# Values held stationary and turned weights streamed, with the weights normalised before their turn, in a six-layer windowed-attention kernel

## The reference, cut to what matters

```
q, k, v = split(shift_tokens(x) @ Wqkv)          # 16 heads of 64
q, k = l2norm(q) * qs, l2norm(k) * ks ; rotary with scale
sim  = einsum('bhwie,bhwje->bhwij', q, k2) * 8   # 8 windows of 32 queries, 64 keys: own window and the one before
attn = softmax(where(mask, -max, sim))
out  = einsum('bhwij,bhwje->bhwie', attn, v2)
x    = out @ Wo + x
x    = (a * gelu(gate)) @ W2 + b2 + x            # of a layer norm of shift_tokens(x), hidden 341
```

## Time and profile before

| quantity | value |
|---|---|
| time, median of 3 runs | 1986.11 us (1985.73 to 1987.9) |
| profiled execution, its own time | 1993.02 us |
| its span | 1991.2 us |
| one full body (start of S0 to the next) | 34.06 us |
| TensorE's granted clock, mean | 0.97 of 2.4 GHz |

### The profile page before, as it was taken

One profiled execution on the slowest core, in us unless ns is written; L12 is line 12 of the kernel. 1 busy time (PEld: TensorE's weight loads), 2 busy tenths in 40 slices (PEclk: granted clock), 3 DMA queues, 4 the chain that ended last, 5 costly groups with the idle time before them and its releaser, 6 DMA issues.

```text
span 1991.2 us, 84866 instructions
## 1 busy us (share of the span) xinstructions
PE 1858.3 (93%) x35408; PEld 1303.1 (65%) x35408; DVE 1589.7 (80%) x3092; ACT 1045.7 (53%) x1879; POOL 903.9 (45%) x1231
## 2 busy tenths in 40 slices
PE   6888858899999999999999999999999999999996
PEld 3444424676767777777767677776767676777674
DVE  5565557788988888888888888888889888888883
ACT  2444423455555656555555556565556555465553
POOL 1000015364554646464555546464645555464640
PEclk7898888999999999999999999999999999999997
DMA  2001006556566656566565666565665646564650
GB/s 69 10 7 64 0 3 100 83 80 102 74 122 109 94 82 94 117 95 108 78 104 72 122 109 94 82 93 117 93 110 76 106 71 124 104 95 83 91 91 22
DMA packets 73332, 166.87 MB, mean 84 GB/s; under 512 B 16592, under 2 KB 23504, under 8 KB 72400
## 3 DMA queue, kind: packets, MB, share of 16 engines
q0 software_dynamic: 36864, 100.71, 37.9%
q1 hardware_dynamic: 36432, 65.68, 12.7%
HBM read 20.57 MB, written 1.05 MB: 11 GB/s over the span
## 4 chain that ended last, share of the span: by engine, by line
PE 69%; DVE 9%; issue 7%; DMA 2%; ACT 0%; DVEq 0%; POOL 0%; POOLq 0%; ACTq 0%
PE ps L997 14%; PE ps L1033 8%; PE ps L1087 7%; PE ps L1107 6%; PE ps L1057 6%; PE ps L1141 5%; PE ps L1009 5%; PE ps L1070 4%; PE ps L1100 3%; DVE big L815 3%; PE ps L1131 3%; PE ps L1021 3%; DVE big L825 2%; DMA big<-big 2%; PE ps L1048 2%
## 5 line engine op out<-in xcount | busy, mean ns | idle before, releaser
L477 POOL DMA_DIRECT2D big<-big x768 | 607.0, 1497 | 62.4 <-DVE big L807 43.9
L564 ACT ACTIVATE big<-ps 128x512 f32<-128x512 f32 x384 | 228.4, 595 | 587.6 <-PE ps L997 540.0
L997 PE MATMUL ps<-big,wn_sb 128*128 128x256 f32 x1536 | 411.2, 396 | 17.5 <-issue 14.9
L815 DVE TENSOR_TENSOR big<-big,ps 128x512 f32<-128x512 f32 x384 | 249.6, 680 | 93.2 <-PE ps L1021 82.8
L997 PEld LDWEIGHTS ps<-big,wn_sb 128*128 128x128 f32 x1536 | 275.4, 192 | 69.6 <-issue 16.5
L468 POOL TENSOR_TENSOR big<-big 128x512 f32<-128x512 f32 x96 | 123.4, 1285 | 360.8 <-ACT big L581 360.8
L804 DVE TENSOR_TENSOR big<-ps,tab 128x512 f32<-128x512 f32 x384 | 262.0, 682 | 11.0 <-ACT big L564 10.9
L807 DVE TENSOR_TENSOR big<-ps,tab 128x512 f32<-128x512 f32 x384 | 259.0, 674 | 0.0
L1141 PE MATMUL ps<-big,wo_sb 128*128 128x256 f32 x768 | 214.5, 382 | 0.0
L443 POOL COPY big<-xs 64x256 f32 x144 | 79.2, 550 | 263.5 <-DVE xs L843 257.6
L1033 PE MATMUL ps<-wn_sb,big 128*64 128x512 f32 x768 | 182.0, 611 | 0.7 <-DVE big L807 0.7
(11 more groups left out here) (146 smaller groups left out, 2917.1 us busy)
## 6 DMA issues: line engine op xcount, KB each, us to landing
big<-big POOLq DMA_DIRECT2D x768, 128.0 KB, 5.0
big<-big SPq DMA_DIRECT2D x96, 256.0 KB
big<-big SPq DMA_DIRECT2D x96, 192.0 KB
wn_sb<-in_wn SPq DMA_DIRECT2D x6, 1024.0 KB, 10.0
wn_sb<-in_wn SPq DMA_DIRECT2D x6, 512.0 KB, 6.1
wo_sb<-in_wo SPq DMA_DIRECT2D x6, 512.0 KB, 4.0
w_sb<-in_w SPq DMA_DIRECT2D x6, 341.0 KB, 3.0
w_sb<-in_w SPq DMA_DIRECT2D x6, 192.0 KB, 3.3
```

Of the source, the lines that this page charges most:

```text
L477: eng.dma_start(rot[to:to + 32, at:at + 4, :], src[32 * r:32 * r + 32], accum_op=ALU.add).then_inc(added[i], 16)
L564: eng.activation(sq[:, two, :], ps[:, i % 2, :].rearrange("p (a t) -> p a t", a=2), ACT.Square).then_inc(sq_d, 1)
L815: eng.tensor_tensor(hat[:, two, :], rot[:, two, :], ps[:, i % 2, :].rearrange("p (a t) -> p a t", a=2), ALU.mult).then_inc(hat_d, 1)
L997: mm = eng.matmul(ps[:, k % 2, a * T:a * T + T], wn_sb[:, u * P:u * P + P], sT, start=True, stop=True)
```

## The change

`W` swaps its operands. A value tile of 64 keys by 64 columns is now stationary, and 32 queries of the turned weights are moving; there are still 32 matmuls a step, now of the shape 64 rows by 64 columns with 32 moving. The result comes out with the head dimension in partitions, as the output projection needs it, so `U` is gone from PE, and `u` evicts banks 5 and 6 straight into `osb` (the rows of `wo` are laid out anew on the host to match). Queries are no longer in partitions behind `W`, so the normalisation moves ahead of the turn: `Y` multiplies the exponentials in place, 1024 elements a partition, and `T` waits for it (`nrm_d`). POOL's `Z` is gone; DVE's `Z` reduces all 16x64 elements. All four lists are new.

```diff
-            S0 F1 k0 k1 S1 k2 F2 T0 k3 T1 k4 g1 W0 W1 k5 T2 k6 T3 F4 k7 U0 U1 g3 W2 W3 V0 V1 V2 V3 U2 O0 O1 F5
-            R0 O2 O3 R1 R2 U3 O4 R3 R4 O5 F6 R5 O6 R6 O7 F7 R7""".split()]
+            k0 k1 S0 k2 k3 F1 S1 g1 k4 k5 T0 F2 T1 k6 W0 W1 k7 V0 g3 F4 O0 O1 T2 T3 O2 W2 W3 V1 V2 V3 R0 O3 R1
+            F5 R2 O4 R3 O5 R4 F6 O6 R5 R6 O7 F7 R7""".split()]
...
-            A0 F0 Z0 m0 Z1 m1 m2 m3""".split()]
+            A0 F0 m0 m1 m2 m3""".split()]
...
                     if kind == "u":
-                        eng.wait_ge(ot_d, it * 4 + (i + 1 - 4))
-                        eng.activation(osb[:, 2 * i:2 * i + 2, :], ps[:, (4, 7)[i % 2], :].rearrange("p (a t) -> p a t", a=2),
+                        eng.wait_ge(ov_d, it * 4 + (i // 2 * 2 + 2 - 4))
+                        eng.activation(osb[:, 2 * i:2 * i + 2, :], ps[:, 5:7, T * (i % 2):T * (i % 2) + T],
                                        ACT.Copy).then_inc(oev, 1)
...
                     if kind == "Z":
-                        eng.wait_ge(den_d, it * 2 + (i - 1 + FREE))
-                        eng.tensor_reduce(den[:, i, :], dn4[:, i, :, :], AX.X, ALU.add).then_inc(den_s, 1)
+                        eng.wait_ge(ex_d, it * 2 + (i - 1))
+                        w = pr_[:, i, :, :].rearrange("p g (r k) -> p (g r) k", r=2)
+                        eng.tensor_reduce(den[:, i, :], w, AX.X, ALU.add).then_inc(den_s, 1)
...
                     if kind == "Y":
-                        eng.wait_ge(ov_d, it * 4 + (2 * i + 2 - 4))
                         eng.wait_ge(rinv_d, it * 2 + (i - 1))
-                        for r in range(2):
-                            scale = rinv[:, i, :].rearrange("p (g r) -> p g r", r=2)[:, :, r:r + 1]
-                            eng.tensor_tensor(on[:, i, :, D * r:D * r + D], ps[:, 5 + r, :].rearrange("p (g d) -> p g d", g=8),
-                                              scale.to_broadcast((P, 8, D)), ALU.mult).then_inc(on_d, 1)
+                        w = pr_[:, i, :, :].rearrange("p g (r k) -> p (g r) k", r=2)
+                        eng.tensor_tensor(w, w, rinv[:, i, :].rearrange("p (a k) -> p a k", k=1).to_broadcast((P, 16, KW)),
+                                          ALU.mult).then_inc(nrm_d, 1)
...
                 def score(c):
                     if c == 0:
-                        eng.wait_ge(on_d, it * 4 + (FREE - 4))
+                        if not (isinstance(it, int) and it <= 1):
+                            eng.wait_ge(oev, it * 4 - 4)
...
                 def turn_weights(q):
                     if q % 2 == 0:
-                        eng.wait_ge(ex_d, it * 2 + (q // 2 - 1))
+                        eng.wait_ge(nrm_d, it * 2 + (q // 2 - 1))
...
                 def weigh(q):
...
-                                mm = eng.matmul(ps[WIN * w:WIN * w + WIN, 5 + r, D * g:D * g + D],
-                                                pts[rows, q, P * a + WIN * w:P * a + WIN * w + WIN],
-                                                v2[rows, win // 2, win % 2, D * p:D * p + D], start=True, stop=True, skip_group_check=True)
+                                    mm = eng.matmul(ps[64 * c:64 * c + 64, 5 + r, T * (q % 2) + at:T * (q % 2) + at + WIN],
+                                                    v2[rows, win // 2, win % 2, D * p:D * p + D],
+                                                    pts[rows, q, T * c + at:T * c + at + WIN], start=True, stop=True, skip_group_check=True)
```

More of the change, by code:

```diff
@@ L235, in gated_flamingo @@
                              "y_d", "r_d", "rb", "hat_d"))
-        sc_d, max_d, sub_d, ex_d, den_d, rinv_d, pt_d, ptev, ov_d, on_d, ot_d, oev, wo_d, x_d, w_go, s_go, vf_free, y2_d, den_h, den_s = (
-            sem(n) for n in ("sc_d", "max_d", "sub_d", "ex_d", "den_d", "rinv_d", "pt_d", "ptev", "ov_d", "on_d", "ot_d", "oev",
+        sc_d, max_d, sub_d, ex_d, den_d, rinv_d, pt_d, ptev, ov_d, nrm_d, oev, wo_d, x_d, w_go, s_go, vf_free, y2_d, den_h, den_s = (
+            sem(n) for n in ("sc_d", "max_d", "sub_d", "ex_d", "den_d", "rinv_d", "pt_d", "ptev", "ov_d", "nrm_d", "oev",
                              "wo_d", "x_d", "w_go", "s_go", "vf_free", "y2_d", "den_h", "den_s"))
@@ L443, in copy @@
                     return eng.tensor_copy(dst, src)
-                for kind, i in share(POOL_PLAN, A, Bh, F, "Am", "Z", "F"):
+                for kind, i in share(POOL_PLAN, A, Bh, F, "Am", "", "F"):
                     if kind == "A":
@@ L619, in _ @@
         def _(eng):
-            for s in (xres, on_d, fx, x_d):
+            for s in (xres, fx, x_d):
                 eng.sem_inc(s, FREE)
@@ L1063, in turn_weights @@
                     if q % 2 == 0:
-                        eng.wait_ge(ex_d, it * 2 + (q // 2 - 1))
-                    if q >= 2:
-                        eng.wait_ge(ptev, it * 4 + (q - 1 - 4))
-                    elif not (isinstance(it, int) and it <= 1):
-                        eng.wait_ge(oev, it * 4 + (q + 3 - 8))
+                        eng.wait_ge(nrm_d, it * 2 + (q // 2 - 1))
+                    if not (isinstance(it, int) and it <= 1 and q < 2):
+                        eng.wait_ge(ptev, it * 4 + (q - 5))
                     for a in range(4):
@@ L1079, in weigh @@
                     if q == 2:
[L1080 removed]
+                        eng.wait_ge(oev, it * 4 + (2 - 4))
                     eng.sem_inc(w_go, 1)
[L1082 to L1083 removed]
+                    for t in range(NT):
                         for w in range(4):
[L1085 to L1101 removed]
+                            for c in range(2):
+                                for r in range(2):
+                                    rows, win, p = slice(64 * r, 64 * r + 64), 4 * t + w, 2 * q + c
+                                    at = P * t + WIN * w
+                                    mm = eng.matmul(ps[64 * c:64 * c + 64, 5 + r, T * (q % 2) + at:T * (q % 2) + at + WIN],
+                                                    v2[rows, win // 2, win % 2, D * p:D * p + D],
+                                                    pts[rows, q, T * c + at:T * c + at + WIN], start=True, stop=True, skip_group_check=True)
+                    mm.then_inc(ov_d, 1)
                 def ffn(s):
@@ L1145, in body @@
                 steps = {"k": project, "g": head_sums, "V": values, "R": spread, "S": score, "T": turn_weights,
-                         "W": weigh, "U": turn_outputs, "O": project_out, "F": ffn}
-                for kind, i in share(PE_PLAN, A, Bh, F, "kgRV", "STWUO", "F"):
+                         "W": weigh, "O": project_out, "F": ffn}
+                for kind, i in share(PE_PLAN, A, Bh, F, "kgRV", "STWO", "F"):
                     steps[kind](i)
@@ L1185, in laid_out @@
         "x": a["x"].reshape(B * T, P), "ctx": a["ctx_1024"].reshape(B * T, P), "xw": xw, "xvec": xvec,
[L1186 removed]
+        "wn": wn, "wo": a[fp + "Wo"].reshape(L, 4, 2, 2, D, P).transpose(0, 2, 4, 1, 3, 5).reshape(L, P, PAIRS, P), "w1": a[fp + "W1"],
         "w2": w2, "vec": vec,
```

39 lines of the change are left out of this document (3 added, 36 removed).

## The result

| | kernel before | kernel after |
|---|---|---|
| median of four runs beside each other | 1987.01 us | 2079.59 us |
| ratio | | 1.0449 (1.0435 to 1.0463) |
| profiled execution, its own time | 1993.02 us | 2078.84 us |
| one full body | 34.06 us | 36.04 us |

The change makes the kernel 4.5% slower. The forecast was 66 us more (2052); the medians differ by 93, the profiled executions by 86.

The account below looks back on a forecast made before the run. A ring through PE and DVE was to bind: 1.74 + 13.40 + 0.14 + 20.05 = 35.33, plus 0.12, 35.45 us a body, 1.4 longer; times 47, 66 us more, 2052. Range 1985 to 2110, likeliest case 2025 to 2085.

Parts of the forecast that it names:

- The ring: PE from k0, DVE from c0 to D3, PE from W0 to the next k0: sets the body at 35.33 us.
- the procedure: Laying the four engines' lists side by side with durations and waits; it gave 33.9 for the earlier body's measured 34.06.
- Z and Y: DVE's 1024-element forms: reduce 1240 ns, multiplication 1200 to 1210 ns; Z adds 1.66 us a body, Y saves 0.14.
- D3 to W0: From the end of DVE's D3 to PE's next matmul: 0.14 us.
- W: On PE, 0.86 us a step instead of 0.72, as loads into different row halves overlap; 0.56 us a body more.
- the tile changes: On PE between W0 and the next k0, six changes of tile shape counted separately: 0.6 us.
- U: PE's transposes U0 to U3 go, 1.74 us a body, but the saving comes back as waits.
- PE alone: Rival: PE alone sets the body and DVE's longer middle is absorbed; 42 us faster, 1944; chance 0.13.
- The slow loads: Rival on W: row-half loads don't overlap, 1.7 a step, 2190; milder, load then stream, 1.28, 2108; chance 0.10 together.
- Cancelling: Rival: ring and saving cancel, with Z and Y at their cheapest; body 34.1 us, about 1986; chance 0.05.

Follow-up runs that it names:

- e1: Kernel after with Y multiplying only 64 of its 1024 elements, waits kept: 2047.01 us, ratio 1.0285 to the kernel before.
- e2: Kernel after with Z reducing 256 elements a partition and adding 1 instead of taking the reciprocal: 2044.03 us, ratio 1.0264 to the kernel before.
- e10: Kernel after with W0's waits reordered, the two for value evictions first and D3's last: 2071.80 us, ratio 1.0398 to the kernel before.
- e6: Kernel before with only W's operands swapped to the new ones (64 value columns stationary, 32 queries moving): 2029.48 us, ratio 1.0207.
- e7: Kernel before with POOL's Z removed and DVE's Z reducing all 1024 elements: 2052.09 us, ratio 1.0319.
- e5: Kernel after with Z and Y both cut to a fraction and W's old operands restored: 2016.70 us, ratio 1.0145 to the kernel before.
- e8: Kernel after with only its lists laid out anew (S0 ahead of k0, F4 and F5 pulled forward): 2220.89 us, ratio 1.1148 to the kernel before.
- e11: Kernel after with other new lists, two function tables a body, Z0 and Y0 together, D2 ahead of d4: 2088.66 us, ratio 1.0486 to the kernel before.
- e3: Kernel after with both cuts together, Y multiplying 64 elements and Z reducing 256 without the reciprocal: 2042.96 us, ratio 1.0268 to the kernel before.

## Why the prediction was right, and where its sizes were off

The sign, the mechanism and the place were right; the size was short by 0.6 us a body (1.4 forecast, 1.98 measured).

- **The ring.** Forecast 1.74 + 13.40 + 0.14 + 20.05 = 35.33, and 0.12 for what the procedure leaves out. Measured 1.70 (`k0` 1009.73 to `c0` 1011.43), 13.50 (to 1024.93), 0.34, 20.50 (1025.27 to 1045.77): 36.04. The first two and their lack of gaps hold. e1 and e2 show that the first 0.8 us taken out of the second comes back in full.
- **Z and Y.** Forecast 1240 and 1205 ns, measured 1209 and 1216. Right.
- **D3 to W0.** Forecast 0.14 from a place with fewer waits behind the late one; measured 0.34, and e10 shows that the order of the waits makes it: 0.2 us a body.
- **W.** This is the term that was mis-sized: 0.86 a step forecast, 1.0 measured, 0.6 a body with the tile changes that I had counted elsewhere. The inference that loads of different row halves overlap held, with a turn 5 ns longer. In the middle of `W0` 17 matmuls are in progress in a window of 0.058 us and 53 in one of 0.58 that begins at the same time: 36 more in 0.522 us, 14.5 ns a pair, four tiles taking 58 ns a turn where I took 53.

```profile
1026.00:1026.06 0.06, 0.06 (x17) 0.06 (x14) 1.00 0.00 0
1026.00:1026.58 0.58, 0.58 (x53) 0.58 (x50) 1.00 0.37 64
```

  64 pairs at 14.5 are 0.93, and the change of tile ahead of a step brings it to 1.0. The rest of that stretch was forecast at 16.61 and is 16.43, since its short waits didn't come.
- **U.** 1.74 us of transposes went, and 2.0 us of PE waits stand in their place at `S1`, `T0` and `W0` (forecast 2.9, with `k5`'s). A ledger of parts that were measured alone, in the kernel before: `W` +0.9 (e6), the sum +1.35 (e7): 36.3, or 34.6 with `U`'s 1.74 saved. It is 36.04, so by this ledger 0.3 of the 1.74 stayed. The ledger is rough: it has no price for `Y`'s move, and in the kernel after the parts don't add (e1 to e5). None of the three orders measured (after, e8, e11) kept the saving, and in e5 the kernel after's own order leaves the body 0.6 us longer than before with `U` gone and nearly all of the new costs gone too.
- **The rivals.** PE alone (1944) is out: PE's waits ahead of `W0` came to 2.0, not under 1. The slow loads (2190, 2108) are out: a step is 1.0, not 1.28 or 1.7. The rule of the Trainium skill (page "TensorE: Matmul & The Clock Gate", "Part 3: Packing small matmuls — row/col tiling") that a load overlaps a matmul in flight only when their row groups differ would have each tile load and stream in turn, 0.020 a pair; 0.0145 was measured, less than that. Two tiles share each row half here, so taken strictly the rule would give more still. Cancelling (1986) is out too: it was to come with `Z` and `Y` at their cheapest, and e3 has them almost free and is still at 1.027, by a second ring that the prediction did not see. For the same reason its 34.1 us a body, for `Z` and `Y` at half their durations, can't be had with these lists and `W` as measured: the floor is 35.2.

What stays open: how the parts of the loss add up in the kernel after. Z, Y and W taken away alone give 0.8, 0.7 and 0.34 us a body, Z and Y together 0.8, all three together 1.3 (e5). The second ring of e3 explains the first two; why `W` gives back no more than a third alone is followed only in part. Open too is what the change saves around a change of layer.

## What to carry to other kernels

Work taken from the fullest engine pays only if the engine it waits for gets no later at the same places: sum the stretch on the second engine between the two points where they meet, and don't go by its busy share (80% here) over the body. Then look for the next ring: here it took over after 0.8 us, however much more of `Z` and `Y` was cut. A reordering that moves a normalisation ahead of its consumer puts its whole latency, reduce, reciprocal and multiply, into the chain, and can make an engine that did part of it in the background (POOL) useless. With several waits at one instruction, put the one that comes last at the end.

## What the runs showed of the hardware that I had not expected

- Small fp32 matmuls are not symmetric in their operands: 64 rows by 32 stationary and 64 moving goes at 1.44 us for 128, 64 by 64 stationary and 32 moving at 2.0, with the same multiplications. In the kernel before that alone is 2.1% (e6). Whether the width of the stationary side or the number of tiles (four instead of eight) makes it, no run separates.
- The order of several waits in front of one instruction has a price: two that had long been met cost 0.24 us behind the late one, 0.34 against 0.10 from `D3` to `W0` (e10), as if they were worked off one by one.
- A change of ACT's function table is 1.28 us, and the order of the list decides how many there are: four a body in e8, two in the kernel after. e8 is 3.0 us a body slower than the kernel after, of which the two loads are 2.56 at most.
